# Gate rows and token numbers loaded by GpSimd in front of each add, with a wait of their own on VectorE

## What is computed

```python
logits = layernorm(x) @ gate_w.T                       # 2048 tokens, 32 experts
top_w, top_idx = top_k(softmax(logits), 8)             # weights divided by their sum
g = silu(einsum('th,ehi->eti', xt, w_gate))            # H = 512, I = 192
u = einsum('th,ehi->eti', xt, w_up)
out = x + sum over e of full_w[t, e] * ((g * u) @ w_down[e])
```

## Time and profile before

| | |
|---|---|
| median of three runs | 763.91 us (759.6 to 767.28) |
| the profiled execution | 759.84 us, its span 758.1 us |
| TensorE (PE) busy | 711.2 us, 94% of the span |
| VectorE (DVE) | 567.0 us, 75% |
| ScalarE (ACT) | 435.4 us, 57% |
| GpSimd (POOL) | 370.7 us, 49% |
| moved by DMA | 179.78 MB, mean 237 GB/s |

### The profile page before, as it was taken

How to read it: one execution, slowest core, us unless ns; L and a number is a source line. 1 busy time by engine, 2 the same in 40 slices (tenths; PEclk the granted TensorE clock), 3 DMA queues, 4 the chain that set the end, 5 groups by cost and what they waited for, 6 DMA issues and landing times.

```text
span 758.1 us, 24471 instructions
## 1 busy us (share of the span) xinstructions
PE 711.2 (94%) x3682; PEld 585.1 (77%) x3683; DVE 567.0 (75%) x1355; ACT 435.4 (57%) x1047; POOL 370.7 (49%) x297
## 2 busy tenths in 40 slices
PE   7999999989778889999999999999999999999994
PEld 5466555656667788889999889899899888898992
DVE  4678888877756477677877877788788778887872
ACT  1665666662035365656666656666676567665652
POOL 2006777767776434443544544434543455344554
PEclk9999999999799999999999999999999999999997
DMA  8996787587898899999999999999999999999995
GB/s 296 350 345 228 275 273 283 214 284 265 282 297 208 178 200 219 212 219 237 217 229 224 238 216 231 221 230 232 234 249 241 233 234 246 248 217 235 218 152 78
DMA packets 174399, 179.78 MB, mean 237 GB/s; under 512 B 36864, under 2 KB 128768, under 8 KB 174368
## 3 DMA queue, kind: packets, MB, share of 16 engines
q0 software_dynamic: 30976, 73.48, 43.1%
q1 hardware_dynamic: 118240, 67.67, 35.4%
q10 hardware_dynamic: 25152, 38.30, 15.5%
HBM read 92.25 MB, written 87.13 MB: 237 GB/s over the span
## 4 chain that ended last, share of the span: by engine, by line
SPq 37%; PE 25%; issue 17%; POOL 7%; DMA 5%; DVE 3%; ACT 2%; ACTq 1%; DVEq 1%; POOLq 0%
SPq L314 24%; SPq L319 7%; POOL x_sorted L506 7%; SPq L433 5%; PE bank L1530 3%; PE bank L1523 3%; PE bank L1524 3%; DMA x_all<-x_sorted 2%; PE bank L1316 2%; DMA x_sorted<-xn_kept,slots 2%; PE bank L1495 1%; PE bank L1347 1%; PE bank L1497 1%; PE bank L1499 1%; PE bank L1496 1%
## 5 line engine op out<-in xcount | busy, mean ns | idle before, releaser
L563 POOL DMA_INDIRECT out_dram<-ctx_all,x_all x144 | 234.5, 1629 | 284.7 <-issue 121.3
L1523 PE MATMUL bank<-gu_hi,xT_hi 128*128 x576 | 194.9, 338 | 1.2 <-ACT xT_hi L791 1.0
L1524 PE MATMUL bank<-gu_lo,xT_hi 128*128 x576 | 195.5, 339 | 0.0
L506 POOL DMA_INDIRECT x_sorted<-xn_kept,slots x96 | 100.7, 1049 | 87.3 <-issue 84.1
L804 ACT ACTIVATE ctx_all<-bank 128x512 f32<-128x512 f32 x144 | 86.0, 597 | 99.8 <-issue 82.6
L1530 PE MATMUL bank<-gu_hi,xT_lo 128*128 x576 | 137.7, 361 | 0.0
L1201 DVE STREAM_TRANSPOSE x_all<-x_all 128x512 f32<-128x512 f32 x146 | 103.9, 712 | 27.9 <-DMA x_all<-x_sorted 23.7
L1248 DVE SCALAR_TENSOR_TENSOR probT<-probT,x_all,bank 128x192 f32<-128x192 f32 x144 | 59.5, 413 | 77.1 <-ACT probT L812 65.5
L1523 PEld LDWEIGHTS bank<-gu_hi,xT_hi 128*128 128x128 f32 x576 | 108.6, 189 | 10.6 <-issue 5.0
L1524 PEld LDWEIGHTS bank<-gu_lo,xT_hi 128*128 128x128 f32 x576 | 108.5, 188 | 5.3
L791 ACT ACTIVATE xT_hi<-x_all 128x512 fp32r<-128x512 f32 x146 | 91.8, 629 | 32.9 <-DVE x_all L1201 32.4
(11 more groups left out here) (222 smaller groups left out, 1112.2 us busy)
## 6 DMA issues: line engine op xcount, KB each, us to landing
x_all<-x_sorted SPq DMA_DIRECT2D x578, 64.0 KB
gu_raw<-in_w_gate_up_dram ACTq DMA_DIRECT2D x28, 768.0 KB
down_raw<-in_w_down_dram ACTq DMA_DIRECT2D x28, 512.0 KB
x_sorted<-pad_rows SPq DMA_DIRECT2D x1, 8720.0 KB, 31.8
x_all<-in_x_dram SPq DMA_DIRECT2D x8, 512.0 KB, 4.9
ctx_all<-in_ctx_dram SPq DMA_DIRECT2D x8, 512.0 KB, 6.9
out_dram<-x_all SPq DMA_DIRECT2D x8, 512.0 KB
gu_raw<-in_w_gate_up_dram SPq DMA_DIRECT2D x4, 768.0 KB
```

Of the source, the lines that this page charges most:

```text
L506: pool.indirect_dma_start(out=x_sorted, out_offset=bass.IndirectOffsetOnAxis(ap=to[:, u, k:k + 1], axis=0), in_=rows[:, u, :], in_offset=N ...
L563: pool.indirect_dma_start(out=out, out_offset=bass.IndirectOffsetOnAxis(ap=xw[:, k, E:E + 1].bitcast(I32), axis=0), in_=y_sb[:, i, :], in_ ...
L1523: pe.matmul(out_gu, xT_hi[:, s, c * P:(c + 1) * P], gate_up(gu_hi, c), start=(c == 0), stop=False)
L1524: pe.matmul(out_gu, xT_hi[:, s, c * P:(c + 1) * P], gate_up(gu_lo, c), start=False, stop=False)
```

## The change

`load_xw` for all tiles from the ninth on moves from SP to GpSimd. GpSimd issues it in `add_tile(j)` for tile j + 4, behind the wait for `y_evac` of tile j (and, at an expert switch, behind the wait for all earlier adds) and directly in front of the add of tile j. The load counts on a semaphore of its own, `xw_loaded[i]`. `xg_loaded[i]` now counts the four x parts only. VectorE gets a wait for `xw_loaded` in front of its wait for silu. The first eight tiles are still loaded by SP and ScalarE, each with a semaphore of its own.

```diff
-    LOADS, BLOCKS = HC + 1, 16
+    LOADS, BLOCKS, AHEAD = HC, 16, 4
...
-        def load_xw(eng, rows, i, block):
+        def load_xw(eng, rows, block, loaded):
-            eng.dma_start(xw[:, bass.ds(block, 1), :].rearrange("p a w -> p (a w)"), rows[:, H:RW]).then_inc(xg_loaded[i], 16)
+            eng.dma_start(xw[:, bass.ds(block, 1), :].rearrange("p a w -> p (a w)"), rows[:, H:RW]).then_inc(loaded, 16)
...
                 load_x_part(sp, rows, i, range(HC))
-                block = k % BLOCKS if type(eight) is int else SLOTS * sp.snap((eight + k // SLOTS) & 1, min_val=0, max_val=1) + k % SLOTS
-                load_xw(sp, rows, i, block)
+                if is_before(eight, k, SLOTS):
+                    load_xw(sp, rows, k, first_xw_loaded[k])
...
                 wait_apart(pool, "pool_passed", (S["y_evac"], j + 1))
+                if type(j) is not int or j >= SLOTS - AHEAD:
+                    pool.reg_load(row_reg, x_row[0:1, bass.ds(j + AHEAD, 1)])
+                    rows = x_sorted[bass.ds(pool.snap(row_reg, min_val=0, max_val=SPARE), P), :]
+                    load_xw(pool, rows, (k + AHEAD) % BLOCKS, xw_loaded[i])
                 pool.indirect_dma_start(out=out, out_offset=bass.IndirectOffsetOnAxis(ap=xw[:, k, E:E + 1].bitcast(I32), axis=0),
...
+                if type(j) is int:
+                    dve.wait_ge(first_xw_loaded[j], 16)
+                else:
+                    dve.wait_ge(xw_loaded[k], 16 * q - 16)
                 dve.wait_ge(S["sil_ready"], j + 1)
```

## The result

The changed kernel takes 858.93 us in the median (855.66 to 867.44, four runs), the kernel before 765.6 us in the same comparison. The ratio is 1.129 with a 95% interval of 1.125 to 1.134. The forecast was 883 us, with 825 to 955 us as its range.

A forecast was written before the change was run, and what follows sets the result against it. TensorE, busy 94%, was taken as the bound, not SP's queue. 759.8 us + 126 for 30 switches - 5 for SP's relief = 881, stated as 883 us to match the median; range 825 to 955 us.

The forecast's parts named there:

- relief of SyncE: SP's queue: one load fewer per tile gains 5 us, at most about 13 us because TensorE idles no more.
- The chain's 37% for SP: Profile page's chain gives SP's queue 37%; the prediction held that SP keeps pace and doesn't hold TensorE up.
- Where the wait falls: At expert switches VectorE's multiplication waits for the new load; about 30 of 31 switches have no window.
- come late less often: Inside an expert: loads were said to be late less often than at switches; no cost was added for them.
- The sum for a switch: Per expert switch: late load +4.85, TensorE's slack -0.8, delayed add +1.26, lighter DMA load -1.1; together 4.2 us, 126 us over 30.
- The slack of TensorE: Between VectorE's multiplication and the transpose that reads it: 0.8 us, taken off each switch's price.
- just fits under the chain: GpSimd's own time per expert, 19.0 us with the loads, stays below the 20.6 us of the chain through the switch.
- The rival's sum: GpSimd as the bound: 14.4 + 4.5 x 1.26 - 1.1 = 19.0 us per expert, 836 us in all; chance 0.10.
- the credit of 1.1: At each switch: DMAs get lighter load as the stage gets longer, so 1.1 us less.
- the heavier case: Rival at switches: loads land in 5.5 us, 6.7 us each, 956 us; idle TensorE may also lose clock; chance 0.05.
- Early landing: Rival: small loads land in 3.0 us or less, so GpSimd's own time decides; 836 us, covering 780 to 850; chance 0.10.
- the faster one: Rival: SP's queue is the real pace and gate rows come in time; 747 to 755 us; chance 0.03.

The follow-up runs named there:

- e9: Against the kernel before: no gate rows loaded by any engine, fixed weights and consecutive token numbers instead; 750.8 us, ratio 0.988.
- e4: Against the kernel before: SyncE still loads all gate rows, but on semaphores of their own, with VectorE's wait at the multiplication; 761.1 us, ratio 0.999.
- e2: Against the change: GpSimd's load for the tile four on is issued in front of the waits for landed adds and y_evac; 809.3 us.
- e6: Against the kernel before: SyncE loads gate rows on own semaphores, and GpSimd makes an equal spare load that nobody reads; 836.3 us, ratio 1.098.
- the fills: SyncE loads gate rows on own semaphores; GpSimd fills 300, 600 or 1200 unused columns per add; ratios to the kernel before 1.009, 1.025, 1.050.

## Why the prediction was right

*What bounds the kernel before.* Right. I allowed 13 us at most for relief of SyncE and took 5; e9 gave 9 with the loads gone, e4 nothing with only the semaphores changed. The chain's 37% for SP was no bound.

*Where the wait falls.* Right at the switch, wrong beside it. The switch above is the one that was described: the load starts behind the landing, VectorE's multiplication waits for it, and TensorE's transpose for that (3.88 us). But I let the switches stand for everything, since inside an expert loads "come late less often". They come late there 55 times of 81, for 97 of the 172.8 us. e2 shows it too: with the switches cured it is still 46 us over the kernel before, though GpSimd's own time is in these too.

*The price.* The sum for a switch doesn't hold, and that 859 us lies near 883 is partly luck. There are 140 loads, not 136, and one takes 0.60 us in place of 0.96, so with the 0.30 in front 0.90 and not 1.26. The largest miss is the landing: I took 4.5 us from scatters, and the loads at switches landed in 2.2 us in the median. The Trainium skill's figure ("DMA: Bandwidth & Descriptors", Anatomy of one DMA, an estimate of 2.04 us) fits there, 2.05 us at 420.80, and not behind an add, where a load took 2.8 to 7.2 us. Adds in front of a switch land 0.7 us sooner (5.2 and 4.5 us behind their end, means), not 1.1. The slack of TensorE before was 1.0 us in the mean at the tiles in question, near my 0.8. With these it is 0.9 + 2.2 + 0.35 - 1.0 - 0.7 = 1.75 us per switch, and 30 x 1.75 = 52.5 us in all. The profile has 19.8 - 16.4 = 3.4 us per expert, 102 us. What the switch price had too much stood in for terms that were missing: late rows inside the experts, GpSimd's own time and the clock.

*GpSimd's own time.* I wrote that it just fits under the chain. It does, by 1.1 us, but it is far from harmless. e6 gives 18.8 us per expert with no late row at all, where the change has 19.8, and is 74 us over the kernel before where the change is 93. The rival's sum, with 0.90 for the load, would have been 14.4 + 4.5 x 0.9 - 1.1 = 17.4 us. What failed is the 0.90, which is 0.98 in e6, and the credit of 1.1: GpSimd idles 5.9 us at a switch of e6 in the mean, against 6.3 before. Without the credit it is 14.4 + 4.5 x 0.98 = 18.8. So the two bounds lie close together, and both must be cured to win much back: more lead alone gives 27 us, the better place 50, both 62, of 93. These gains don't add up, so no share of the 93 us belongs to one cause alone.

*What would show it.* GpSimd's load takes 0.6 us, not 1; TensorE's busy share in the windows is 85 to 89%, not near 80; the DMA share is 0.86 to 0.89 as said. A load that lands within 2 us was to shrink the price, and at the switches it took about that. The clock isn't free either, and the sum had nothing for it, only the heavier case: 0.98, 0.93, 0.95 and 0.98 are granted from 300 to 700 us where it was 1.00. Between the first and the last switch TensorE has half its clock for 47.6 us, which is the work of 24 us at full clock, and had it for 6.8 us before. The four runs of the change go the same way: spans of 865.7, 858.6, 855.6 and 853.9 us at mean clocks of 0.953, 0.961, 0.968 and 0.972. How much of it reaches the time wasn't tested.

*The rivals.* Early landing had the landing right at the switches (under 3.0 us at 28 of 31) and the place wrong: behind an add it isn't early, and 836 us is 23 us under the measured time. The heavier case was not the time, and the faster one was refuted by e9: without any gate rows the kernel is at 751 us.

## What to carry to other kernels

An engine with a mean share of 49% had little free of every 16.4 us, because it spent much of the rest waiting for its own DMAs to land. I counted 2 us; by the fills it was some 0.15 us for each tile, 0.7 us for an expert. Look at what an engine does between two such waits before giving it work. A load that is needed early must not stand behind a wait for something else: here the same load, issued in front of the wait, cost 50 us less. And count lead in tiles from the point where the issuing engine really is, backlog included, not from the tile's number.

## What was not expected of the hardware

- A plain DMA of 128 rows of 132 bytes, issued by GpSimd, keeps it for 0.60 us, a scatter of 128 rows for 0.96. From issue to landing its 16.5 KB took 2.0 to 3.5 us where all adds had landed, and 2.8 to 7.2 us inside an expert, where an add of 256 KB had been issued just before.
- A fill by GpSimd starts before the add in front of it has ended in the profile: its row is 1.21 us long where it stands behind an add and 0.60 where it stands alone (600 columns), and it costs 0.50 us. A load behind the wait costs 0.98. The same holds for e2, where a load right behind an add has a row of 1.22 us.
- Taking all gate rows from SyncE, four loads per tile in place of five, brought 1.2%, though SyncE's queue led the chain with 37%.
- TensorE's clock fell to its lower level eleven times between the first and the last switch of the change. Each time TensorE was idling at L1490, or had done so less than 2 us earlier, for 1.9 to 4.3 us. It was at the lower level for 47.6 us in all, where the kernel before had 6.8.
